# Three bias vectors enter as bf16 products on TensorE instead of additions on GpSimd, in a fused transformer, state-space and mixture block

## What is computed

```python
mod = (_silu(L0_c) @ L0_wmod).reshape(L0_c.shape[0], 6, 1, -1)
sa, ca, ga, sb, cb, gb = (mod[:, 0], mod[:, 1], mod[:, 2], mod[:, 3], mod[:, 4], mod[:, 5])
h = _layernorm(x, axis=-1) * (1 + ca) + sa
# inside: xn = LN(h); causal attention with 16 heads -> attn_out @ o_w + o_b; a selective state-space
# scan (512 inner channels x 16 states over 512 tokens) -> ssm_out; then
#   x = h + alpha * attn_out + (1.0 - alpha) * ssm_out
#   return x + gelu(LN(x) @ ffn_w1 + ffn_b1) @ ffn_w2 + ffn_b2
x = x + ga * attn_ref(h, ...)
h = _layernorm(x, axis=-1) * (1 + cb) + sb
# inside: h @ base_w.T + base_b + 2 * (two of 8 low-rank experts, chosen by a router)
x = x + gb * ffn_ref(h, ...)
```

## Time and profile before

| what | us |
|---|---|
| median of 3 runs | 5944.29 (5938.65 to 5945.28) |
| the profiled execution, its own time | 5941.06 |
| its span in the profile | 5938.9 |
| PE busy | 5262.0 (89%) |
| DVE busy | 5103.3 (86%) |
| ACT busy | 4094.7 (69%) |
| POOL busy | 4194.8 (71%) |

### The profile page before, as it was taken

One profiled execution on the slowest core, in us unless ns is written; L12 is line 12 of the kernel. 1 busy time (PEld: TensorE's weight loads), 2 busy tenths in 40 slices (PEclk: granted clock), 3 DMA queues, 4 the chain that ended last, 5 costly groups with the idle time before them and its releaser, 6 DMA issues. The chain is left out here.

```text
span 5938.9 us, 115651 instructions
## 1 busy us (share of the span) xinstructions
PE 5262.0 (89%) x32280; PEld 3518.1 (59%) x32280; DVE 5103.3 (86%) x7776; ACT 4094.7 (69%) x6407; POOL 4194.8 (71%) x2545
## 2 busy tenths in 40 slices
PE   4799989989898898989989899898988989899986
PEld 2466655656565566656566556565655666565664
DVE  3898889888899898998989898898998989989983
ACT  3677767767776766767767777677767667677763
POOL 3678767767677677776777677676776777767772
PEclk7899999999999999999999999999999999999997
DMA  4444444444454444454444444444444444444441
GB/s 129 132 140 142 140 148 149 142 128 142 135 152 147 129 142 128 144 152 135 143 126 140 144 151 143 127 141 133 152 148 126 142 133 143 151 142 137 142 129 39
DMA packets 521726, 814.74 MB, mean 137 GB/s; under 512 B 80432, under 2 KB 227288, under 8 KB 520976
## 3 DMA queue, kind: packets, MB, share of 16 engines
q1 hardware_dynamic: 513072, 805.79, 44.4%
q10 hardware_dynamic: 7904, 0.39, 0.1%
HBM read 716.50 MB, written 88.38 MB: 136 GB/s over the span
## 5 line engine op out<-in xcount | busy, mean ns | idle before, releaser
L584 POOL TENSOR_TENSOR state<-scan_in,bc 128x1024 f32<-128x1024 f32 x1024 | 2405.9, 2362 | 650.6 <-PE pY L940 504.2
L1201 DVE TENSOR_TENSOR_SCAN pD<-pD,state 128x512 f32<-128x512 f32 x1536 | 1851.2, 1216 | 190.1 <-ACT pD L708 119.9
L708 ACT ACTIVATE pD<-scan_in,A 128x512 f32<-128x512 f32 x2048 | 1397.5, 690 | 656.5 <-DVE state L1209 572.6
L940 PE MATMUL pY<-ident,state 128*128 128x128 f32 x8192 | 1214.0, 282 | 102.9 <-DVE state L1209 94.8
L940 PEld LDWEIGHTS pY<-ident,state 128*128 128x128 f32 x8192 | 928.6, 145 | 335.7 <-DVE state L1209 145.8
L1209 DVE TENSOR_TENSOR state<-pD,bc 128x512 f32<-128x512 f32 x1536 | 1024.6, 680 | 44.7 <-issue 24.6
L1259 DVE TENSOR_REDUCE mx<-pM 128x1 f32<-128x512 f32 (+3 forms) x1408 | 850.3, 630 | 69.8 <-PE pM L1030 67.5
L809 ACT ACTIVATE region<-pM 128x512 f32<-128x512 f32 (+1 forms) x1408 | 733.6, 556 | 255.3 <-PE pM L1048 224.8
L571 POOL TENSOR_TENSOR state<-state,bc 128x512 f32<-128x512 f32 x512 | 644.2, 1273 | 342.9 <-DVE state L1201 333.4
L1201 DVE TENSOR_TENSOR_SCAN state<-pD,state 128x512 f32<-128x512 f32 x512 | 606.0, 1207 | 105.0 <-ACT pD L708 105.0
L1046 PE MATMUL pM<-region 98*128 98x512 bf16 (+3 forms) x2048 | 535.5, 310 | 101.5 <-DMA region<-mrow 45.0
(11 more groups left out here) (171 smaller groups left out, 8360.6 us busy)
## 6 DMA issues: line engine op xcount, KB each, us to landing
bc<-bc_d SPq DMA_DIRECT2D x2048, 256.0 KB, 4.0
region<-qk_d SPq DMA_DIRECT2D x640, 128.0 KB, 3.6
qk_d<-qkp SPq DMA_DIRECT2D x64, 384.0 KB, 2.6
qk_d<-ht SPq DMA_DIRECT2D x64, 384.0 KB, 3.1
xt<-in_x_dram SPq DMA_DIRECT2D x32, 512.0 KB, 5.7
hres_d<-xt SPq DMA_DIRECT2D x32, 512.0 KB, 5.1
region<-qk_d SPq DMA_DIRECT2D x256, 64.0 KB, 3.0
x<-hres_d SPq DMA_DIRECT2D x32, 512.0 KB, 5.9
```

What stands on the lines that cost most here:

```text
L584: nc.gpsimd.tensor_tensor(state[:, at_:at_ + JP], us[:, parity(b), k // N * JP:(k // N + 1) * JP, :], bc[:, k % BC_SLOTS, 0, :].unsqueeze( ...
L708: act.activation(pD[DECAY_BANK[e]][:], dts[:, parity(b), j], ACT.Exp, scale=A[:, j, n:n + 1]).then_inc(a_ok.sem, 1)
L940: ins = pe.matmul(y_part(t, e % JP), state[:, e % RING, t * P:(t + 1) * P], ident[:], is_transpose=True, start=False, stop=(e % PASS >= PA ...
L1201: v.tensor_tensor_scan(h if e in POOL_C else decay, decay, h, 0.0, ALU.mult, ALU.add)\
```

## The change

The three additions on POOL go. Before each of `sso0`, `sso1`, `f2_0`, `f2_1`, `out0` and `out1` PE gets one more matmul, `bias_row`: a stationary operand of ones with 3 rows and 128 columns times a moving operand of 3 rows and 512 columns in bf16, the bias vector split into three bf16 parts. `base_b` is no longer multiplied with gb beforehand, since it now enters before the gate, and `mod_rows` has six blocks instead of seven (one DMA of 128 KB per turn less, in `xr`). The residual is stored from `ht`; the layer norm `l1a` writes to `xt` instead of in place, `xt` feeds the transposes, and the load of the next `x` waits for these transposes. The DVE makes the three parts once, at the start of the program.

```diff
@@ setup (DVE)
-            link(v.tensor_tensor(ob_row[:], ob_row[:], alpha, ALU.mult))
+            link(v.tensor_tensor(bias_f[0:3, 0], bias_f[0:3, 0], alpha[0:3], ALU.mult))
+            link(v.tensor_copy(bias_hi[0:3], bias_f[0:3]))
+            link(v.tensor_tensor(bias_left[0:3], bias_f[0:3], bias_hi[0:3], ALU.subtract))
+            link(v.tensor_copy(bias_mid[0:3], bias_left[0:3]))
+            link(v.tensor_tensor(bias_left[0:3], bias_left[0:3], bias_mid[0:3], ALU.subtract))
+            link(v.tensor_scalar(bias_left[0:3], bias_left[0:3], ident[0:3, 2:3], None, ALU.mult))
+            link(v.scalar_tensor_tensor(out=bias_left[0:3], in0=bias_mid[0:3], scalar=ident[0:3, 1:2],
+                                        in1=bias_left[0:3], op0=ALU.mult, op1=ALU.add))
+            link(v.scalar_tensor_tensor(out=bias_rows[0:3], in0=bias_hi[0:3], scalar=ident[0:3, 0:1],
+                                        in1=bias_left[0:3], op0=ALU.mult, op1=ALU.add))
@@ SP
                 elif name == "load":
-                    b.wait_last(sp, hres_out)
+                    sp.wait_ge(built, CLEARED)
+                    b.wait_last(sp, xt_ps)
...
-                    sp.dma_start(hres_d[b.index].rearrange("(t p) f -> p t f", p=P), xt[:]).then_inc(hres_out.sem, 16)
+                    sp.dma_start(hres_d[b.index].rearrange("(t p) f -> p t f", p=P), ht[:]).then_inc(hres_out.sem, 16)
...
                 elif name == "x1p":
-                    sp.wait_ge(built, CLEARED)
-                    b.wait(sp, hres_out)
                     b.wait_last(sp, x2_ok, 1)
...
-                    for a, col in ((0, 2), (1, 5), (2, 6)):
+                    for a, col in ((0, 2), (1, 5)):
@@ POOL
-                elif name == "l0c":
-                    b.wait(pool, h_made, 2)
-                    nc.gpsimd.tensor_tensor(xt[:], ht[:], row(ob_row[:]), ALU.add).then_inc(h_made.sem, 1)
...
-                elif name == "f1_0":
-                    b.wait(pool, n2)
-                    nc.gpsimd.tensor_tensor(x1[:], x1[:], row(f2b_row[:]), ALU.add).then_inc(x1b.sem, 1)
...
-                elif name == "xb":
-
-                    b.wait(pool, n3)
-                    nc.gpsimd.tensor_tensor(xr, xr, row(mod_g[:, 2, :]), ALU.add).then_inc(xb_ok.sem, 1)
@@ ACT
-                    normalise(b, 1, ht, ht, n1)
+                    normalise(b, 1, xt, ht, n1)
...
+                        if n == 1:
+                            b.wait(act, hres_out)
                         b.wait_last(act, qk_out[n % 2])
@@ PE
+            def bias_row(ps, n):
+
+                pe.matmul(ps[:], ones_row[0:3, :], bias_rows[0:3, n, :].unsqueeze(1).broadcast_to([3, 2, D]),
+                          start=True, stop=False, skip_group_check=True)
...
                     ps = next_bank(name, b, r_ok, n + 1)
+                    bias_row(ps, 1)
                     for t in range(2):
                         for f in range(FT):
                             ins = pe.matmul(ps[:, t * D:(t + 1) * D], gT(b)[:, f, (2 * n + t) * P:(2 * n + t + 1) * P],
-                                            w_f2[:, f, :], start=(f == 0), stop=(f == FT - 1))
+                                            w_f2[:, f, :], start=False, stop=(f == FT - 1),
+                                            skip_group_check=True)
@@ DVE
                 elif name[:3] == "f2_":
                     n = int(name[3])
                     b.wait(dve, f2_ps, n + 1)
-                    b.wait(dve, x1b)
@@ ORDER["PE"], its first entries
-        z3 mt0 add19 -f2_0 +xt0 -f2_1 mx1_0 add20 +xt1 st0_0_0 mx1_1 add21 add22 st0_0_1 st0_0_2 +qk0 st0_0_3
+        add19 -f2_0 +xt0 -f2_1 +xt1 st0_0_0 st0_0_1 mx1_0 add20 st0_0_2 mx1_1 add21 add22 st0_0_3 st0_1_0 +qk0
```

More of the change, by code:

```diff
@@ L264, in adaln_block @@
         rt_raw = view(D)
-        mods = view(7 * D)
-        bb_row = view(D)
+        mods = view(6 * D)
+        bias_f, bias_left = (view(3 * D).rearrange("p (n f) -> p n f", n=3) for _ in range(2))
+        bias_hi, bias_mid = (view(3 * D // 2, BF16).rearrange("p (n f) -> p n f", n=3) for _ in range(2))
         alpha = view(D)
@@ L1364 @@
     "SP": """
-        -rb22 -rb25 -rb23 -ld3 -rc23 -rb24 -mt2 -rc25 -rb26 -rc24 -rb27 -x1p -rc26 -rc28 -rb28 -rb29 -rc27 xp
-        -rb30 ld0 -mt3 -rb31 -rc30 -rc29 -rc31 +load rb1 rb0 rc0 rc1 rc2 rb2 rb3 rc3 rb4 ld2 rc4 rb5 rc5 rb7 rb6
-        rb8 rb9 rc8 rc6 rc7 ld1 rb10 rc10 rc9 rb11 rb12 rc12 rb13 rc13 rc14 -xr rc11 rc15 mt0 rb15 rc16 rb16 rb14
-        +qk0 +qk1 rb18 rc17 +qk2 rb20 rb17 rc18 +l1a rb19 mt1 rc20 rb21 +qk3 rc21 -put rc19 rc22
+        -rc23 -x1p -rb28 -mt2 -rc26 -rb26 -rb27 -rc25 xp ld0 -rb31 -rc27 -rb29 -rc28 -mt3 -rb30 rb1 rb0 -rc29
@@ L1369 @@
+        -rc30 rc0 rb2 -rc31 rb3 rc2 rc1 rb4 rc3 +load rc4 rb7 rb5 rc5 rb6 rb8 ld1 rc6 ld2 rc8 rb10 rb9 rc7 rc10
+        rc9 rb12 -xr rb11 rc11 rc12 rb15 rb13 rb14 rc13 +l1a rc14 rc16 rc15 mt0 +qk0 rb19 rb16 +qk1 rc17 rb17
+        rb18 rc18 +qk2 rb20 rc19 mt1 rb22 +qk3 rb21 rc20 rc21 rc22 -put rb23 ld3 rb25 rb24 rc24
     """,
     "POOL": """
-        fill8 fill9 pc14 -f1_0 pc15 +l0s fill10 +l0a fill11 +l0b +l0c +l1s fill12 pc22 pc23 fill13 -x2 -x2b -l3s
-        +ql0 fill14 -xb +ql1 fill15 +ql2 fill16 pc30 pc31 fill17 +ql3 -gb fill18 -put fill19 fill20 fill21 pc38
@@ L1375 @@
+        +fill3 +fill4 +pc6 +pc7 +fill5 +fill6 l2s +fill7 +fill8 +fill9 +pc14 +pc15
     """,
     "ACT": """
-        z0 dec5 dec6 dec7 dec8 dec9 dec10 dec11 z1 dec12 dec13 -l2a dec14 -h2t0 -h2t1 dec15 z2 dec16 dec17 -f1_0
-        -f1_1 dec18 -f1_2 -f1_3 dec19 -f1_4 dec20 +l0a -f1_5 dec21 -f1_6 -f1_7 dec22 -gelu mt0 dec23 dec24 z3
-        dec25 +l1a zsilu dec26 dec27 st0_0_0 +xt0 +xt1 st0_0_1 dec28 st0_0_2 +qk0 dec29 st0_0_3 st0_1_0 st0_1_1
-        +qm0 -l3a st0_1_2 +qk1 -h3t0 -h3t1 +qm1 +qk2 dec30 dec31 +xs0 +qm2 +xs1 st0_1_3 +qk3 st0_2_0 +qm3 -route2
@@ L1388 @@
+        dec55 st2_3_0 dec56 oe2 dec57 st3_0_0 st3_0_1 st3_0_2 dec58 st3_0_3 st3_1_0 dec59 +sp2 st3_1_1 dec60
+        st3_1_2 st3_1_3 st3_2_0
     """,
     "PE": """
-        z3 mt0 add19 -f2_0 +xt0 -f2_1 mx1_0 add20 +xt1 st0_0_0 mx1_1 add21 add22 st0_0_1 st0_0_2 +qk0 st0_0_3
-        add23 st0_1_0 add24 add25 st0_1_1 mx1_2 mx1_3 +qk1 st0_1_2 -h3t0 -h3t1 +qk2 -route st0_1_3 +xs0 +xs1 +qk3
-        st0_2_0 pv0_0 pv0_1 st0_2_2 -lora add26 st0_3_0 add27 -axt mx1_4 mx1_5 -out0 mx1_6 -out1 mx1_7 mx1_8
@@ L1398 @@
-        st2_1_3 pv2_0 mt3 st2_2_0 st2_2_2 pv2_1 st2_3_0 add50 pv2_2 pv2_3 st3_0_0 st3_0_1 st3_0_2 add51 add52
-        add53 st3_0_3 st3_1_0 on2 add54 add55 st3_1_1 add56 +mx0_0 +mx0_1 add57 st3_1_2 st3_1_3 pv3_0 add58 add59
-        st3_2_0 st3_2_2 st3_3_0 pv3_1 pv3_2 pv3_3 +v0 on3 +v1 add60 ot0 add61 add62 ot1 add63 +z0 yt0 +skip0
-        +add0 yt1 yt2 +add1 yt3 +add2 +add3 sso0 sso1 +add4 +add5 +z1 +add6 +mx0_2 +add7 +add8 +add9 +mx0_3
-        +add10 +add11 +z2 h2t0 h2t1 +add12 +add13 f1_0 f1_1 f1_2 f1_3 f1_4 +mx0_4 f1_5 f1_6 f1_7 +add14 +mx0_5
@@ L1403 @@
-        +mx0_6 +mx0_7 +add15 +mx0_8 +add16 +mx0_9 +add17 +mx0_10 +add18
+        add19 -f2_0 +xt0 -f2_1 +xt1 st0_0_0 st0_0_1 mx1_0 add20 st0_0_2 mx1_1 add21 add22 st0_0_3 st0_1_0 +qk0
+        st0_1_1 add23 add24 st0_1_2 add25 mx1_2 add26 mx1_3 +qk1 -h3t0 -h3t1 +qk2 -route +xs0 +qk3 st0_1_3 +xs1
+        pv0_0 st0_2_0 pv0_1 st0_2_2 -lora st0_3_0 add27 -axt mx1_4 mx1_5 -out0 mx1_6 -out1 mx1_7 mx1_8 add28
+        mx1_9 mx1_10 mt1 add29 pv0_2 mx2_0 pv0_3 add30 add31 st1_0_0 st1_0_1 st1_0_2 skip1 st1_0_3 mx2_1 add32
@@ new lines @@
+        st3_0_3 st3_1_0 +mx0_0 add55 st3_1_1 +mx0_1 st3_1_2 add56 add57 st3_1_3 pv3_0 add58 add59 st3_2_0 st3_2_2
+        pv3_1 st3_3_0 pv3_2 pv3_3 +v0 on3 add60 +v1 ot0 ot1 add61 add62 add63 +z0 yt0 +skip0 yt1 yt2 yt3 +add0
+        +add1 +add2 +add3 sso0 sso1 +add4 +add5 +z1 +add6 +mx0_2 +add7 +add8 +add9 +add10 +mx0_3 +z2 +add11 h2t0
+        h2t1 +add12 +add13 f1_0 f1_1 f1_2 f1_3 f1_4 f1_5 +mx0_4 f1_6 f1_7 +mx0_5 +add14 +add15 +add16 +mx0_6
+        +mx0_7 +mx0_8 +add17 +mx0_9 +mx0_10 +add18 +z3 +mt0
@@ L1404 @@
     """,
     "DVE": """
-        c16 c17 +l0s scan18 c18 scan19 mx0_4 c19 scan20 c20 scan21 c21 mx0_5 mx0_6 mx0_7 mx0_8 mx0_9 mx0_10
-        scan22 +l1s scan23 scan24 mt0 scan25 c24 c25 -f2_0 scan26 -f2_1 c26 mx1_0 mx1_1 scan27 c27 -l3s +qk0
-        mx1_2 mx1_3 +qk1 scan28 c28 scan29 c29 +qk2 -route +xs0 scan30 +qk3 +xs1 -lora scan31 scan32 mx1_4 mx1_5
-        c32 scan33 mx1_6 c33 scan34 mx1_7 mx1_8 mx1_9 mx1_10 c34 mt1 scan35 mx2_0 c35 gate0 scan36 scan37 c36 c37
-        mx2_1 scan38 scan39 scan40 scan41 c40 mx2_2 c41 scan42 mx2_3 c42 +xs2 mx2_4 scan43 mx2_5 c43 mx2_6 on0
@@ new lines @@
+        scan22 scan23 scan24 c24 scan25 c25 scan26 scan27 mt0 c26 -f2_0 c27 -f2_1 mx1_0 -l3s +qk0 mx1_1 mx1_2
+        scan28 mx1_3 c28 scan29 +qk1 c29 scan30 +qk2 -route +xs0 +qk3 +xs1 -lora scan31 mx1_4 scan32 mx1_5 c32
+        scan33 mx1_6 c33 scan34 mx1_7 mx1_8 mx1_9 mx1_10 c34 mt1 scan35 mx2_0 c35 gate0 scan36 scan37 c36 c37
```

(2 more changed lines are left out.)

110 lines of the change are left out of this document (56 added, 54 removed).

## The result

The changed kernel takes 6159.95 us (median of 5 runs, 6155.65 to 6161.70) against 5944.29 (5938.65 to 5953.93, 5 runs). The ratio is 1.036, 95% interval 1.0349 to 1.0371. The forecast was 5987 us, the range 5925 to 6040: the direction was right, but of the 216 us of loss 43 were foreseen. The profiled execution has a span of 6158.1 us, 219.2 more than before.

A forecast was written before the change was run, and what follows sets the result against it. PE's work was taken to bound most of a turn, ACT and DVE the rest. Products 42, chain minus 13, setup 5 and jumps 9 summed to plus 43 us on 5944.3: 5987 us, range 5925 to 6040 (forecast's own 5955 to 6015).

The forecast's parts named there:

- Products: Six added bias matmuls a turn on PE's path, 0.22 us each: 1.3 us a turn, plus 42 us.
- banks: PE's waits for DVE at `mx0` and `mx1` go, waits for ACT replace them: zero, 1.3 us a turn either way.
- chain: Behind `f2_1`, `add26` fills PE's wait for ACT at `h3t0`: minus 0.4 us a turn, minus 13 us.
- jumps: PE's and ACT's stalls at 13 loop jumps move but keep their size: plus 9 us, bounds minus 51 and plus 21.
- SP: Transfers: ACT's `qk1` wait for the stored residual free, `x` load has time, one 128 KB DMA fewer: nothing.
- The upper bound of 2.3 us a turn: Six products on PE at a whole matmul duration of 0.38 us each, against 1.3 us a turn taken.
- the clock's bound: Upper bound of the jumps' term, slower PE clock after ACT's stall included: plus 21 us instead of plus 9.
- The additions: Removing 7.1 us a turn from POOL gains nothing, as PE's work hides POOL; without that cover, 3.1 us a turn.
- ACT's jump costs more: Rival: ACT's stall in its busy part delays `pv3_2`, `ud`, `skip0`, clock falls twice: 72 us more, 6059; chance 0.17.
- My corners: Parts of a turn between `add44`, `mx1_7` on PE and `mx1_7`, `c44` on DVE: same steps; PE gains at most 6.6 us.
- The setup: Seven more DVE operations ahead of its first `bn_stats`, on the path: plus 5 us, between 3 and 7.

The follow-up runs named there:

- e3: The changed kernel without its six bias products a turn, so three biases are missing from the output: 6056.52 us, ratio 1.019.
- e2: The old steps, with the three POOL additions and no products, in the changed kernel's order and banks: 6049.20 us, ratio 1.0175.
- e1: The changed steps (products on PE, no POOL additions, residual from the modulated tile) in the order and banks of the kernel before: 6017.95 us, ratio 1.0116.
- e10: e1 with each bias product issued twice in a row, so that the biases enter the sums twice: 6046.17 us, ratio 1.0174.
- e11: The kernel before with 14 turns in the loop's body, 2 iterations and one jump back: 5803.00 us, ratio 0.976.
- e17: e1 with 14 turns in the loop's body: 5884.67 us, ratio 0.9891.
- e4: The changed kernel with SP's loads of `xr` moved six rows later, behind `rc16`: 6098.70 us, ratio 1.0251.
- e13: The changed kernel with SP's order of the kernel before, all other lists and the banks as changed: 6091.14 us, ratio 1.0244.
- e7: The changed kernel with SP's `x1p` (load of the residual, 512 KB) behind `mt2` instead of ahead of it: 6136.32 us, ratio 1.0318.
- e9: The kernel before with SP's `xr` four rows earlier, behind `rb12`: 5961.53 us, ratio 1.0023.
- e15: The kernel before with SP's `xr` four rows later, behind `rc16`: 5989.32 us, ratio 1.0081.

## Why the prediction was wrong

Taken apart by the runs, the loss of 216 us is: the changed steps 82, the order in turns without a jump 71 (both with one jump), and 12 jumps that are dearer by (6160.0 - 5955.5) / 12 - (5945.2 - 5803.0) / 12 = 17.0 - 11.9 = 5.1 us, 62 in all. That sums to 215. The parts depend on the order in which they are counted: the products are dearer in the new order (e3), and the new steps make the new order's jumps dearer (e2).

That PE's work bounds most of a turn was right; the sizes were not. Products stood at 42 us, banks and chain together at minus 13, jumps at 9 and SP at nothing; the runs give about 77, plus 71 and 62. The step that failed first is the price of the new order: that it could lose no more inside the parts than the banks' 1.3 us a turn (it lost 2.4), and that a jump's stall keeps its size wherever it stands. The second is the price of a product.

**The products**, forecast at 1.3 us a turn and 42 in all, cost 2.5 and 80 (e1). The mechanism was right: all six lie on the path. The size was off. I took 0.22 us "since the number of columns is the same", from one row's distance to the next start. e10 shows that this is the price only behind another product; the first of a pair costs 0.42. The upper bound of 2.3 us a turn was nearer, and still too low. It would also have put the end of the forecast's own range at 5987 + 31 = 6018, and with the clock's bound at 6030, not at 6015. Three rows did not make the product cheap: in the pairs of e10 it takes 0.22 us to the next start, as the product with 98 rows did. This agrees with the rule that the prediction quotes from the Trainium skill, TensorE: Matmul & The Clock Gate, section "Why this matters for your kernels". Both bounds missed the 0.2 us around the product.

**The additions** at nothing: right to within 0.4 us a turn (e2 against e3); from e11 to e17 PE's idle time changes by 0.3. Their cover was there.

**The jumps** failed, and with them **SP**, whose part ended "Nothing". I priced PE's and ACT's jumps and left out DVE's, although its 1.9 us stood among the waits of before. And I took a stall's size as fixed ("the stalls go where the jumps go and keep their size"). The runs show that it depends on what SP issued just before. In the changed kernel `xr` comes 3.2 us ahead of DVE's stall, which is 4.2 us instead of 1.9. Behind a DVE stall of 2 us PE waits 1.1 us in `f1`, behind one of 4 us 3.5. e4 takes that transfer away and wins 61 us, e13 restores the old SP order and wins 69. The count of DMAs, which I did give, says nothing; their place does. The other items came about as priced: in the turn shown ACT's stall in the last head group is 1.86 us and PE waits 2.08 behind it, PE's own is 5.0 on average, and `z1` is free of its wait. `x1p` ahead of `mt2` adds 2.0 us, again by SP's order: in a jump turn PE's `mt2` and `mt3` are 26.1 us apart, and 24.0 in e7. The 2.4 us more in `f1` and these 2.0 make up most of the 5.1 us by which a jump is dearer. The rival "ACT's jump costs more" gave 6059 for another reason than the one that the runs show.

That the stalls keep their size was my reading of the rule, which gives no size. The Trainium skill, Runtime: NRT & Kernel Launch, section "Instruction fetch mechanics", also says that the sequencer fetches through a DMA queue of its own. The traces agree: their DMA records show one 16 KB packet of an instruction queue that starts in a PE stall or just ahead of it (in 196 of the 197 stalls of all runs). The packet takes 1.0 us in both kernels and 1.1 in e4, and PE goes on 2.5 to 2.9 us after its start (averages of the runs). What differs is its start: 2.4 us into the stall in both kernels, 0.5 in e9 and 1.0 in e4 and e15. So the fetch is not slower behind `xr` or the store; it begins later.

**The banks**, "zero, with 1.3 us a turn either way": the exchange of a wait for DVE against one for ACT came true, and as a sum it stayed near zero (1.9 us before, 2.1 after). But longer waits of `st` and `add` came on top, and PE idles 1.5 us a turn more in all. Whether the lists or the banks lose it, no run separates. The remaining 1.0 us a turn of PE's busy time is not settled either: the granted clock is 0.98 in both windows. My corners showed the same steps in each part; that a new order inside a part can lose more than the banks' 1.3 us, I did not price.

**The chain behind `f2_1`**: the wait at `h3t0` did shrink, from 0.64 to 0.31 us, which is lost among the rest. **The setup**: `x2` of the first turn starts at 361.4 us, 5.2 later than 356.2, and 5 was forecast.
